# One-hot products with exchanged operands, ScalarE factors, a dummy gather and VectorE roots in a routed expert kernel

## The reference

```python
logits = xf @ gate_W.T
pi = _sinkhorn(-logits)                    # 20 rounds over 4096 x 8
_, top_idx = jax.lax.top_k(pi, TOP_K)      # TOP_K = 2
y = einsum(silu(xf W_gate) * (xf W_up), W_down)   # per expert
out = sum over k of y[top_idx[:, k]] * pi[:, k]
```

## Time and profile before

| what | value |
|---|---|
| median of 3 runs | 2640.54 us |
| the profiled execution | 2636.76 us |
| its span | 2635.0 us |
| mean granted TensorE clock | 0.951 |
| busy: PE, VectorE, ScalarE, GpSimd | 93%, 63%, 42%, 36% |

### The profile page before, as it was taken

How to read it: one execution, slowest core, us unless ns; L and a number is a source line. 1 busy time by engine, 2 the same in 40 slices (tenths; PEclk the granted TensorE clock), 3 DMA queues, 4 the chain that set the end, 5 groups by cost and what they waited for, 6 DMA issues and landing times. The chain is left out here.

```text
span 2635.0 us, 53432 instructions
## 1 busy us (share of the span) xinstructions
PE 2444.0 (93%) x16410; PEld 2218.5 (84%) x16410; DVE 1655.2 (63%) x3864; ACT 1109.1 (42%) x2287; POOL 942.6 (36%) x2146
## 2 busy tenths in 40 slices
PE   1779999999999999999999999877779999999998
PEld 1669889989989989989989989865669989998887
DVE  7456666666666666666666566437766766676554
ACT  2334434334334334334334334235434555555443
POOL 3124344334334334334334334210023443344432
PEclk9689999999999999999999999875669999999999
DMA  4311111111111111111111111259934444454341
GB/s 153 113 24 25 32 32 24 32 32 24 32 31 24 32 31 25 32 31 25 32 29 27 32 28 25 61 174 300 295 113 164 171 165 161 156 174 162 136 131 22
DMA packets 229914, 218.04 MB, mean 83 GB/s; under 512 B 130012, under 2 KB 204128, under 8 KB 220640
## 3 DMA queue, kind: packets, MB, share of 16 engines
q1 hardware_dynamic: 177360, 185.63, 22.4%
q0 software_dynamic: 11232, 29.18, 3.8%
q10 hardware_dynamic: 41264, 2.51, 1.0%
HBM read 164.52 MB, written 54.53 MB: 83 GB/s over the span
## 5 line engine op out<-in xcount | busy, mean ns | idle before, releaser
L629 DVE TENSOR_TENSOR w_lo<-w_raw,w_hi 128x512 fp32r<-128x512 f32 x288 | 190.0, 687 | 4.0
L1216 POOL TENSOR_SCALAR xrow_v<-bag 128x1 f32<-128x1 f32 x32 | 7.2, 224 | 509.4 <-DVE bag L1734 509.4
L760 PE MATMUL ps_back<-w_hi,eh_hi 128*128 128x256 f32 x624 | 180.1, 289 | 3.1 <-DVE eh_lo L639 3.1
L760 PE MATMUL ps_back<-w_lo,eh_hi 128*128 128x256 f32 x624 | 176.5, 283 | 0.0
L760 PE MATMUL ps_back<-w_hi,eh_lo 128*128 128x256 f32 x624 | 176.5, 283 | 0.0
L718 ACT ACTIVATE w_hi<-w_raw 128x512 fp32r<-128x512 f32 x288 | 169.8, 626 | 9.0 <-DMA w_raw<-wts_d 9.0
L1721 DVE TENSOR_TENSOR oT<-oT 128x512 f32<-128x512 f32 x64 | 44.3, 693 | 175.0 <-ACT oT L1380 175.0
L730 ACT ACTIVATE sact<-ps_inva 128x512 f32<-128x512 f32 (+1 forms) x96 | 49.7, 517 | 236.1 <-PE ps_inva L760 236.1
L1363 ACT ACTIVATE yi<-ps_invb 128x512 f32<-128x512 f32 x128 | 71.2, 623 | 183.6 <-PE ps_invb L1917 183.5
L1923 PE MATMUL ps_back<-state,kqT_t 128*128 128x128 f32 x1024 | 133.9, 286 | 11.0 <-DVE la L1745 11.0
L1591 DVE SCALAR_TENSOR_TENSOR aP<-ps_front,nbh,dT 128x256 f32<-128x256 f32 x256 | 111.2, 480 | 41.6 <-PE ps_front L1869 41.6
(11 more groups left out here) (372 smaller groups left out, 7222.1 us busy)
## 6 DMA issues: line engine op xcount, KB each, us to landing
w_raw<-wts_d SPq DMA_DIRECT2D x72, 1024.0 KB, 5.6
wts_d<-prep SPq DMA_DIRECT2D x96, 256.0 KB, 3.8
dT<-alphaT_d SPq DMA_DIRECT2D x32, 512.0 KB, 3.8
prep<-L_ffn_W_gate_dram SPq DMA_DIRECT2D x32, 256.0 KB, 3.3
prep<-L_ffn_W_up_dram SPq DMA_DIRECT2D x32, 256.0 KB, 3.8
prep<-L_ffn_W_down_dram SPq DMA_DIRECT2D x32, 256.0 KB, 4.5
x_all<-L_attn_x_dram SPq DMA_DIRECT2D x4, 1024.0 KB, 9.7
hTr<-hT_d SPq DMA_DIRECT2D x32, 128.0 KB, 2.0
```

The lines of the kernel that those rows point to most:

```text
L629: V.tensor_tensor(piece(w_lo[p], m).bitcast(F32R), piece(w_raw, m), piece(w_hi[p], m), ALU.subtract).then_inc(split[n], 1)
L760: ins = MM(out_, w[a].bitcast(F32R), x[b].bitcast(F32R), start=start and n == 0, stop=stop and n == 2)
L1216: link(pool.tensor_scalar(xrow_v[:, 0:1], bag[:, 1:2], LN_EPS, None, ALU.add), x_pool, n)
```

## The change

- The pair products have their operands exchanged: `col_hot` is stationary and `lane_hot` moves, so the list comes out as 78 x 128. VectorE copies it to SBUF (`listT`), PE transposes it, and the rest reads it from there.
- VectorE no longer multiplies by the token number. It writes `col_hot` first and `lane_hot` second; ScalarE scales `col_hot` in place, 8 instructions of 128 x 78 a batch, before it loads its Silu table and splits the first weights.
- The loops over batches in VectorE's and PE's programs are written out.
- GpSimd issues one dummy indirect gather (128 rows, all of row 0) after its tables, long before the first real one, and waits for it before that one.
- SyncE waits for the first slot's gathered rows before it loads the second slot's weights.
- The three roots of the last tile are made by VectorE.

```diff
@@ -324,9 +325,11 @@
         lane_hot = [k_s[:, n].rearrange("p (n l) -> p n l", n=PAIRS_B) for n in range(2)]
         col_hot = [a[:, 0:PAIRS_B * ETILES * RB].rearrange("p (n l) -> p n l", n=PAIRS_B) for a in (y4, v_s)]
         numbers = g_s[:, 0:P]
+        repeated = lambda a: a.unsqueeze(1).to_broadcast([P, PAIRS_B, a.shape[1]])
         tokens = g_s[:, P:P + TILES * TOPK]
         xf_rows, out_rows = xf_d.rearrange("t p d -> (t p) d"), out.rearrange("b s d -> (b s) d")
         dec_flat, COLS = dec[:, :, :].rearrange("p t n -> p (t n)"), ETILES * RB
+        listT = q_s[0:COLS, 0:P]
         token_f, pad_f = dec_flat[:, 0:COLS], dec_flat[:, COLS:2 * COLS]
         which = dec_flat[:, 2 * COLS:4 * COLS].rearrange("p (c k) -> p c k", k=TOPK)
         dest_i = dec_flat[:, 4 * COLS:5 * COLS].bitcast(I32)
@@ -334,7 +337,8 @@
         sk_dve, sk_act, sk_pe = sem("sinkhorn_dve"), sem("sinkhorn_act"), sem("sinkhorn_pe")
         rt_dve, rt_pe, pi_ready = sem("routing_dve"), sem("routing_pe"), sem("pi_ready")
         te_ready = sem("te_ready")
-        tables_made, pairs_dve, pairs_ready, pairs_used = (sem(n) for n in ("tables_made", "pairs_dve", "pairs_ready", "pairs_used"))
+        tables_made, pairs_used, lanes_ready, cols_made, cols_ready = (sem(n) for n in ("tables_made", "pairs_used", "lanes_ready", "cols_made", "cols_ready"))
+        pos_ready, warm_index, warmed, listT_ready, entries_filled = (sem(n) for n in ("pos_ready", "warm_index", "warmed", "listT_ready", "entries_filled"))
         list_ready, ridx_ready, list_dve = sem("list_ready"), sem("ridx_ready"), sem("list_dve")
 
         pool_turn, sp_turn, dve_turn, pe_turn = sem("pool_turn"), sem("sp_turn"), sem("dve_turn"), sem("pe_turn")
@@ -591,25 +595,20 @@
             ch.link(V.tensor_scalar(pos_col, pos_all, 1 / P, -(P - 1) / (2 * P), ALU.mult, ALU.add))
             ch.link(V.tensor_scalar(pos_col, pos_col, ROUND, None, ALU.add))
             ch.link(V.tensor_scalar(pos_col, pos_col, -ROUND, None, ALU.add))
-            ch.link(V.scalar_tensor_tensor(pos_lane, pos_col, -float(P), pos_all, ALU.mult, ALU.add))
+            V.scalar_tensor_tensor(pos_lane, pos_col, -float(P), pos_all, ALU.mult, ALU.add).then_inc(pos_ready, 1)
+            dve.wait_ge(pos_ready, 1)
             dve.wait_ge(tables_made, 2)
-            def hots(b, p, first):
-                if not first:
+
+            for b in range(BATCH):
+                pairs = slice(b * PAIRS_B, (b + 1) * PAIRS_B)
+                if b >= 2:
                     dve.wait_ge(pairs_used, b - 1)
-                pairs = bass.ds(b * PAIRS_B, PAIRS_B)
-                repeated = lambda a: a.unsqueeze(1).to_broadcast([P, PAIRS_B, a.shape[1]])
-                ch = Chain(dve, pairs_dve, b)
-                V.tensor_tensor(lane_hot[p], repeated(numbers), per_head(pos_lane[:, pairs], P), ALU.is_equal)
-                ch.link(V.tensor_tensor(col_hot[p], repeated(numbers[:, 0:ETILES * RB]), per_head(pos_col[:, pairs], ETILES * RB), ALU.is_equal))
-                V.tensor_tensor(col_hot[p], col_hot[p], per_head(tokens[:, pairs], ETILES * RB), ALU.mult).then_inc(pairs_ready, 1)
-
-            for p in range(2):
-                hots(p, p, True)
-            with dve.Fori(1, BATCH // 2) as i:
-                for p in range(2):
-                    hots(2 * i + p, p, False)
+                V.tensor_tensor(col_hot[b % 2], repeated(numbers[:, 0:COLS]), per_head(pos_col[:, pairs], COLS), ALU.is_equal).then_inc(cols_made, 1)
+                V.tensor_tensor(lane_hot[b % 2], repeated(numbers), per_head(pos_lane[:, pairs], P), ALU.is_equal).then_inc(lanes_ready, 1)
             dve.wait_ge(pairs_used, BATCH)
-            entry = psB[1][:, 0:COLS]
+            V.tensor_copy(listT, psB[1][0:COLS, 0:P]).then_inc(listT_ready, 1)
+            dve.wait_ge(entries_filled, 1)
+            entry = psB[0][:, 0:COLS]
             ch = Chain(dve, list_dve)
             ch.link(V.tensor_scalar(token_f, entry, -1.5, 0.5, ALU.add, ALU.mult))
             ch.link(V.tensor_scalar(token_f, token_f, ROUND, None, ALU.add))
@@ -741,6 +740,12 @@
 
             for c in range(QD + QS, QN):
                 act_prepare(act, 0, c)
+            act.wait_ge(tables_made, 2)
+            for b in range(BATCH):
+                act.wait_ge(cols_made, b + 1)
+                for n in range(PAIRS_B):
+                    ins = A(col_hot[b % 2][:, n, :], col_hot[b % 2][:, n, :], ACT.Copy, scale=tokens[:, b * PAIRS_B + n:b * PAIRS_B + n + 1])
+                ins.then_inc(cols_ready, 1)
             act.preload_act_table_set("silu_and_others")
             for m in range(PIECES):
                 high(m, 0, 0)
@@ -785,17 +790,14 @@
             for c in range(QD + QS + 2, QN):
                 pe_prepare(pe, 0, c)
 
-            def pairs(b, p, first=False, last=False):
-                pe.wait_ge(pairs_ready, b + 1)
+            for b in range(BATCH):
+                pe.wait_ge(lanes_ready, b + 1)
+                pe.wait_ge(cols_ready, b + 1)
                 for n in range(PAIRS_B):
-                    ins = MM(psB[1][:, 0:ETILES * RB], lane_hot[p][:, n, :], col_hot[p][:, n, :], start=first and n == 0, stop=last and n == PAIRS_B - 1)
+                    ins = MM(psB[1][0:COLS, 0:P], col_hot[b % 2][:, n, :], lane_hot[b % 2][:, n, :], start=b == 0 and n == 0, stop=b == BATCH - 1 and n == PAIRS_B - 1)
                 ins.then_inc(pairs_used, 1)
-
-            pairs(0, 0, first=True), pairs(1, 1)
-            with pe.Fori(1, BATCH // 2 - 1) as i:
-                for p in range(2):
-                    pairs(2 * i + p, p)
-            pairs(BATCH - 2, 0), pairs(BATCH - 1, 1, last=True)
+            pe.wait_ge(listT_ready, 1)
+            nc.tensor.transpose(psB[0][:, 0:COLS], listT, ident[0:COLS, 0:COLS]).then_inc(entries_filled, 1)
 
             def rows_T(j, p, rows, gathers):
                 pe.wait_ge(xrow_loaded[p], 16 * gathers)
@@ -853,9 +855,15 @@
 
             pool.wait_ge(back_evac[BU_LG % 2], b_evac(TILES, BU_LG))
             pool.sem_inc(pool_turn, 1)
+            pool.memset(ridx[:, 0, 0:1], 0).then_inc(warm_index, 1)
             pool.iota(numbers, pattern=[[1, P]], base=0, channel_multiplier=0, allow_small_or_imprecise_dtypes=True).then_inc(tables_made, 1)
             pool.iota(tokens.rearrange("p (t k) -> p t k", k=TOPK), pattern=[[TOPK * P, TILES], [1, TOPK]], base=1, channel_multiplier=TOPK, allow_small_or_imprecise_dtypes=True).then_inc(tables_made, 1)
 
+
+            pool.wait_ge(x1_stored, 16 * 2)
+            pool.wait_ge(warm_index, 1)
+            pool.sem_inc(pool_turn, 1)
+            pool.indirect_dma_start(xin[:, 0, :], None, out_rows, bass.IndirectOffsetOnAxis(ap=ridx[:, 0, 0:1], axis=0)).then_inc(warmed, 16)
 
             def gather_rows(j, p, rows, column):
                 n = rows // P
@@ -909,6 +917,7 @@
 
             pool.wait_ge(xf_stored, 16 * TILES + 16)
             pool.sem_inc(pool_turn, 1)
+            pool.wait_ge(warmed, 16)
             pool.wait_ge(pi_stored, 16)
             pool.wait_ge(list_ready, 1)
             pool.sem_inc(pool_turn, 1)
@@ -960,6 +969,7 @@
 
             sp.wait_ge(te_ready, 1)
             load_weights(0, 0, True)
+            sp.wait_ge(xrow_loaded[0], 16 * BB)
             load_weights(1, 2 * BIG)
             with sp.Fori(1, SMALL) as i:
                 load_weights(2 * i, 2 * i)
@@ -1275,9 +1285,6 @@
                 for p in range(2):
                     step(2 * i + p + 1, 1 - p, True, True)
             step(TILES - 1, 1, False, True)
-            o_roots(TILES - 1, 1)
-            m_root(TILES - 1)
-            x_root(TILES - 1)
             pool_late(pool)
 
 
@@ -1800,8 +1807,29 @@
             step(TILES - 3, 1, True, True, True)
             step(TILES - 2, 0, True, False, True)
             step(TILES - 1, 1, False, False, True)
-            for part in (tail_o, tail_xln, tail_x2, tail_m, tail_fc, tail_x1, tail_xf, tail_logits):
-                part(TILES - 1)
+            ch = Chain(dve, last_dve)
+            dve.wait_ge(os_ready, TILES)
+            dve.wait_ge(ss_ready, 2 * TILES)
+            ch.link(V.tensor_scalar(qe[:, :], ssq[:, 1, :], DK * RMS_EPS, DK * RMS_EPS * RMS_EPS, ALU.mult, ALU.add))
+            ch.link(V.scalar_tensor_tensor(os_[:, 1, :], os_[:, 0, :], 1.0 / DK, qe[:, :], ALU.mult, ALU.add))
+            root(ch, os_[:, 1, :], or_[:, 0, :], or_[:, 1, :])
+            dve.sem_inc(or_ready, 1)
+            tail_o(TILES - 1)
+            tail_xln(TILES - 1)
+            tail_x2(TILES - 1)
+            dve.wait_ge(mv_ready, TILES)
+            ch.link(V.tensor_scalar(mrow_v[:, 1:2], mrow_v[:, 0:1], 1.0 / D, RMS_EPS, ALU.mult, ALU.add))
+            root(ch, mrow_v[:, 1:2], mrow_r[:, 0:1], mrow_r[:, 1:2])
+            dve.sem_inc(mr_ready, 1)
+            tail_m(TILES - 1)
+            tail_fc(TILES - 1)
+            tail_x1(TILES - 1)
+            dve.wait_ge(xv_ready, TILES)
```

(6 more changed lines are left out.)

## The result

The changed kernel takes 2624.19 us (median of 4 runs, 2623.12 to 2628.39), the kernel before in the same rounds 2641.86 (4 runs, 2636.68 to 2644.23): ratio 0.9934, 95% interval 0.9914 to 0.9955. Forecast were 2623.8 us and 16.7 us less in the profiled execution; that went from 2636.76 to 2623.29 us, 13.5 less, its span from 2635.0 to 2621.6. Timed again later beside other versions, the changed kernel took 2623.67 us (6 runs), ratio 0.9946 (0.9929 to 0.9964).

A forecast was written before the change was run, and what follows sets the result against it. From the last tile's tail to the first expert slot, a chain of waits across engines was taken to bound the kernel. Gains 4.0 + 1.2 + 7.2 + 3.7 + 0.6 = 16.7 us, from 2640.5 to 2623.8; full range 2616 to 2634.

The forecast's parts named there:

- Late roots: Last tile's tail: m and x roots on VectorE instead of GpSimd each save 2.0 us, 4.0 us together.
- The clock in the tail: Fully connected products: a shorter root wait may keep PE's clock up, gaining 0 to 2.3 us, taken as 1.2.
- The o root at 0: Last tile's first root: quicker on VectorE, but hidden behind a store that ScalarE awaits, so gain 0.
- Pairs, 7.2 us: List of pairs: exchanged operands raise the clock, ScalarE scales; 8.0 us gained, 0.8 paid for copy and transpose, net 7.2.
- rival A: Pairs: clock stays at 0.50, so the stage gains nothing and pays 0.8 us; total gain 8.7, 2631.8 us; chance 0.20.
- ScalarE's split behind the list at 0: First expert weights: ScalarE's split moves behind its last scaling but finishes before the gathered rows come; cost 0.
- Iterations at 0: Balancing iterations after the tail: start 5.2 us earlier and keep that whole gain, with no loss to the DMA rings.
- The wait on SyncE: Gather: holding back the second slot's weights frees the rings, so PE gets the rows 3.7 us sooner.
- The dummy gather: Gather: an earlier dummy spares the first real one a slower first use; 0 to 1.0 us, taken as 0.6.
- Rival B: Iterations: early start lost to busy DMA rings, 2.5 us or more of the tail's 5.2 lost; 2628 us; chance 0.08.
- rival C: Pairs: ScalarE's scaling binds and the kernel gets slower, from 0.59 us a copy; 2641.8 us at 0.63; chance 0.04.

The follow-up runs named there:

- run 9: Changed kernel with the last tile's o root alone back on GpSimd, m and x roots staying on VectorE; 2629.55 us (one run).
- run 6: Changed kernel without the dummy gather and GpSimd's wait for it; 2620.51 us (one run).
- run 1: Changed kernel with the pair products' operands not exchanged (128 columns stationary, 78 moving), without copy and transpose; 2628.4 us, ratio 0.9956.
- run 2: Changed kernel with pair operands not exchanged, moving column one-hots padded from 78 to 128 columns, no copy or transpose; 2630.73 us (one run).
- run 4: Changed kernel with three buffers instead of two for each one-hot; 2615.64 us, ratio 0.9923; timed again 2618.52 us, ratio 0.9917.
- run 3: Changed kernel with VectorE multiplying by the token factors again, no scaled copies on ScalarE, operands still exchanged; 2624.08 us (one run).
- run 7: Changed kernel with all three roots of the last tile (o, m, x) back on GpSimd; 2632.54 us, ratio 0.9965.
- run 10: Changed kernel with three buffers for each one-hot and the o root back on GpSimd; 2616.35 us, ratio 0.9911.

## Why the forecast was right

The sign and most of the time came from the mechanisms that I had named. That the number fits so closely is in part luck. By the traces, without the attention phase, the gain is 16.0 us for 16.7, but the errors of the terms are larger and cancel: 2.2 us too little for the clock in the tail and 1.4 for a store, against 1.6 too much for the pairs, 0.9 for the o root, 0.5 for the dummy and 1.5 for the iterations, which scatter. And the forecast of 2623.8 rests on a median of 2640.54 for the kernel before, which was 2641.86 in the rounds of the result and 2638.54 in the last ones.

- **Late roots, 4.0 us: right.** 2.01 and 2.03 us; GpSimd for m alone gives the 2.0 back.
- **The clock in the tail, 1.2 us: too small.** It stayed up for the fully connected products (-2.5 us), the two transposes ahead of them (-0.25) and the router's transposes and products (-0.66): 3.4 us. My range ended at 2.3, and had only the first of these. With m alone on GpSimd they take 5.21, so 1.4 us of it are this root's; how long the clock stays low behind the same stop differs by run (6.35, 5.47 and 5.21 us for stops of 2.89 to 2.91 us).
- **The o root at 0: wrong in kind.** I followed only the chain of waits: hidden behind a store. That it is, but an operation that ends early in front of a wait moves PE's work away from the work behind the wait, and then the clock, low already, comes back 6.2 us into that work and not 1.3. Cost 1.5 us, by run 9. Between before and after it shows as 0.9 us only (projection 5.89 us before, 6.77 after), as PE had a stop of 1.02 us there before, too.
- **The store in the tail: not forecast.** ScalarE gets it 9.0 us from the sum of squares, before 10.5: 1.4 us less. In eleven of the twelve other traces of versions of the changed kernel, with the roots on either engine, it is 8.8 to 9.6, so the roots don't do it; in the twelfth (run 6) it is 10.6, as late as before. With one trace of the kernel before, this can't be told from scatter: that the change gains the 1.4 us is not shown.
- **Pairs, 7.2 us: right in mechanism, 1.6 too much.** The clock rose in the second batch, as forecast, and rival A did not come; run 1 against the first trace shows that the exchange does it: same content, same 78 columns, other operand moving. The forecast named the moving width from one stream of the tail; run 2 bears it out. Mis-sized were three terms. ScalarE's copies are 0.25 us apart and not 0.21, 2.10 a batch and not 1.85. A batch keeps PE 1.94 us from its first product to its last at the high clock, and not 1.7, which is near the pace of batches that touch (1.75 apart in run 4) but not what a buffer waits for. Both lie in the loop of two buffers: 5.08 us for 4.6. And the first product starts 3.22 us after the first one-hot, not 2.84 (0.81 + 0.09 + 2.17 and a hand-over). From it to the list it is 21.6 us, where I had named under 21. Copy and transpose cost 0.7 (0.8 forecast). The Trainium skill (ScalarE: Activation LUTs, section "What ACT_TABLE_LOAD costs") has the figures from which 0.25 us apart was estimated. The trace agrees: (2.11 - 0.34) / 7 = 0.25, so here the estimate from the page was better than my reading of the earlier trace rows, where I had scaled four copies of 128 columns down to 78.
- **ScalarE's split behind the list at 0: right.** It ends 4.9 us after the first list operation, VectorE's half at 1929.0, and VectorE still waits 2.0 us for the first rows to split.
- **Iterations at 0: right within the scatter** of 125.9 to 128.2 us, which leaves room for a loss of about 1 us.
- **The wait on SyncE, 3.7 us: right.** 3.68 by the traces, 3.5 by taking it out.
- **The dummy gather, 0.6 us: wrong, nothing.** I had read 1.49 against 0.95 us as a first use. The changed kernel shows 1.31 and 1.47 for the first two real gathers, with the dummy long done, and its wait for the dummy costs the 0.1 us that the issues gain.
- **Rival B** (early start lost to the rings) did not come: it was to take back 2.5 us or more, and the nine early traces average 1.1 us more than the three latest; **rival C** (ScalarE binds and loses) neither: at 0.25 us a copy it is far from 0.59.

## What to carry to other kernels

When a stage runs at the low clock though PE is 100% busy, try the operands the other way round, with the wider one moving: here that was worth 6 us in 31, copy and transpose paid. Before an operation is moved to a faster engine, see what PE work it sets free and what follows: work that PE does early, ahead of a wait, no longer stands directly before the work behind the wait, and here the clock then came back later and 1.5 us were lost. And where a stage passes through three engines, count the loop of a buffer and not each engine's time: with two buffers two batches took 5.08 us, with three 4.0, and the third buffer brought about 4 us where the relief of VectorE brought 0.9 at most.

## What the runs showed of the hardware

- Products of fp32 one-hots with 128 moving columns went from granted clock 0.50 to 1.00 with a stationary of 78 columns as of 128; with 78 moving columns and a stationary of 128 they stayed at 0.50 for 27 us at 100% busy PE. At 0.50 one batch starts 3.41 us behind the other before the change and in run 1, and 3.46 exchanged, so the exchange gives nothing at the same clock.
- A slower feed did not bring it down again: with gaps of 0.75 us between batches of 1.94 (run 3), and of 1.5 between batches of 2.02 (run 2), the clock stayed at 1.00 to the end of the products.
- The fully connected products took 3.84 us behind a stop of PE of 0.88 us, and 5.2 to 6.35 us behind one of 2.9.
- With the clock at 0.50 at its start, the output projection took 4.36 to 5.01 us directly behind eight transposes (runs 7, 9 and 10), and 6.77 us behind the same transposes and a stop of 3.09 us (changed kernel).
- An indirect gather's issue on GpSimd takes 0.95 to 1.5 us, the first two of a slot's four the longer ones, with or without a dummy before.
